# Attention: two PSUM banks for score tiles and four for chunks, the maxima of two chunks in one VectorE instruction

## What is computed

```python
# layer 0
h = _sln(hidden, w, ...)                      # layer norm, scaled and shifted by a condition
q, k, v = ...(h @ Wqkv.T + bqkv)              # 16 heads of width 32
energy = jnp.einsum('bhqd,bhkd->bhqk', q, k)
att = jax.nn.softmax(energy, axis=-1) / D ** 0.5
out = jnp.einsum('bhqk,bhkd->bhqd', att, v)
h1 = out @ Wp.T + bp + hidden
# layer 1: weights rounded to -1, 0, 1 and activations to 8 bits in the projections
attn = jax.nn.softmax(jnp.einsum('bhqd,bhkd->bhqk', q, k) * hd ** (-0.5), axis=-1)
o = jnp.einsum('bhqk,bhkd->bhqd', attn, v)
x = x + bitlinear(o, w_proj, b_proj)
x = x + bitlinear(gelu(bitlinear(adaln(x), w_fc1)), w_fc2)
```

## Time and profile before

| | |
|---|---|
| time, median of 3 runs | 2861.51 us (2854.57 to 2863.14) |
| the profiled execution | 2858.09 us |
| its span | 2856.3 us |
| TensorE products busy | 2659.4 us, 93% of the span |
| weight loads busy | 1494.5 us, 52% |
| VectorE busy | 2204.9 us, 77% |
| ScalarE busy | 1844.1 us, 65% |
| GpSimd busy | 1962.6 us, 69% |
| mean granted TensorE clock | 0.976 |

### The profile page before, as it was taken

One profiled execution on the slowest core, in us unless ns is written; L12 is line 12 of the kernel. 1 busy time (PEld: TensorE's weight loads), 2 busy tenths in 40 slices (PEclk: granted clock), 3 DMA queues, 4 the chain that ended last, 5 costly groups with the idle time before them and its releaser, 6 DMA issues. The chain is left out here.

```text
span 2856.3 us, 61816 instructions
## 1 busy us (share of the span) xinstructions
PE 2659.4 (93%) x22219; PEld 1494.5 (52%) x22273; DVE 2204.9 (77%) x4467; ACT 1844.1 (65%) x3329; POOL 1962.6 (69%) x1571
## 2 busy tenths in 40 slices
PE   7899899999999999999759998999899899959998
PEld 5655466554765547555325554554455455524444
DVE  5778678776888768877677768776878688749998
ACT  4366555665556645566456677667766776658997
POOL 0389724896269952799438987998789799965442
PEclk9999999999999999999979999999999999989999
DMA  6122443223432415223222314322332222252001
GB/s 229 39 58 63 149 123 101 58 69 133 140 94 57 121 70 166 70 62 95 74 78 60 77 32 115 80 57 45 102 79 60 69 76 58 50 205 97 33 29 38
DMA packets 102196, 243.54 MB, mean 85 GB/s; under 512 B 18828, under 2 KB 25108, under 8 KB 101016
## 3 DMA queue, kind: packets, MB, share of 16 engines
q1 hardware_dynamic: 100120, 233.49, 28.9%
q0 software_dynamic: 1792, 6.33, 0.6%
HBM read 99.15 MB, written 38.88 MB: 48 GB/s over the span
## 5 line engine op out<-in xcount | busy, mean ns | idle before, releaser
L502 DVE TENSOR_REDUCE a_mxs<-ps 128x1 f32<-128x512 f32 x2048 | 1268.5, 681 | 256.7 <-PE ps L371 254.3
L463 ACT ACTIVATE a_p<-ps 128x512 f32<-128x512 f32 x2048 | 1042.6, 607 | 202.5 <-PE ps L385 192.2
L342 POOL TENSOR_TENSOR a_sum<-a_p 128x512 f32<-128x512 f32 x768 | 985.3, 1292 | 127.3 <-PE ps L403 104.9
L371 PE MATMUL ps<-a_k,a_q 96*128 96x512 f32 x2048 | 855.0, 424 | 27.9 <-DVE a_mxs L502 24.3
L385 PE MATMUL ps<-a_q,a_k 98*128 98x512 f32 x2048 | 810.4, 419 | 18.6 <-ACT a_p L463 12.4
L347 POOL TENSOR_TENSOR a_sum<-a_sum,a_p 128x512 f32<-128x512 f32 x512 | 663.5, 1296 | 40.1
L403 PE MATMUL ps<-a_sum,a_unit 128*32 128x512 f32 x1536 | 656.4, 598 | 14.8 <-POOL a_sum L347 12.0
L403 PE MATMUL ps<-a_p,xv 128*32 128x512 f32 x3968 | 645.0, 598 | 1.4 <-DVE tok L521 1.4
L371 PEld LDWEIGHTS ps<-a_k,a_q 96*128 96x128 f32 x2048 | 388.9, 190 | 262.8 <-DVE a_mxs L502 108.8
L385 PEld LDWEIGHTS ps<-a_q,a_k 98*128 98x128 f32 x2048 | 384.2, 189 | 256.2 <-ACT a_p L463 161.7
L472 ACT ACTIVATE a_ots<-ps 128x512 f32<-128x512 f32 x256 | 152.6, 598 | 415.9 <-PE ps L403 414.7
(11 more groups left out here) (251 smaller groups left out, 3121.9 us busy)
## 6 DMA issues: line engine op xcount, KB each, us to landing
a_q<-qh SPq DMA_DIRECT2D x256, 128.0 KB, 2.3
a_k<-kh SPq DMA_DIRECT2D x256, 128.0 KB, 2.4
a_q<-ql SPq DMA_DIRECT2D x128, 128.0 KB, 2.3
a_k<-kl SPq DMA_DIRECT2D x128, 128.0 KB, 2.4
x<-a_p SPq DMA_DIRECT2D x64, 256.0 KB, 2.1
a_p<-in_w_fc SPq DMA_DIRECT2D x12, 1024.0 KB, 8.0
kh<-in_x SPq DMA_DIRECT2D x4, 2048.0 KB, 14.3
a_p<-x SPq DMA_DIRECT2D x16, 512.0 KB, 6.3
```

Source lines behind the costliest of these rows:

```text
L342: pair = pool.tensor_tensor(tile, self.key_tile(u, kt), self.key_tile(u, kt + 1), ALU.add)
L371: pe.matmul(self.mx[self.mx_ring[at]], self.q[j][0:96, t * P:(t + 1) * P], self.k[j][0:96, half * HALF:(half + 1) * HALF], start=True, sto ...
L463: act.activation(self.key_tile(u, kt), self.st[self.st_ring[CHUNKS * k + n]], ACT.Exp, scale=self.scale).then_inc(self.s_exp, 1)
L502: dve.reduce_max(self.mxs[:, k % 2, c:c + 1], self.mx[self.mx_ring[CHUNKS * k + c]], axis=AX.X).then_inc(self.s_mxr, 1)
```

## The change

The scores get two banks (0 and 1) in place of three, and each tile alternates. The chunks get four (2 to 5). The first 28 chunks of a batch still go round three of them (5, 3, 4), the later ones round all four, so that the two chunks of a step lie in neighbouring banks, 2 and 3 or 4 and 5. For those VectorE issues one reduction of a step's two chunks (`reduce_chunks`): it waits until both are there, reads 128 x 2 x 512 values across both banks, writes two columns of `mxs`, and raises `s_mxr` by two. It stands where the first of the two reductions stood, so in steps 2 (odd heads) and 6 the `divide` that stood between two reductions now stands behind the joint one. The reductions of the prelude stay single. `MX_CREDIT` grows to 32, since the bank that the early chunks don't use was last used 32 chunks ago.

```diff
--- before.py
+++ after.py
@@ -40,11 +40,12 @@
 NQ = H // NJ
 STEPS = 8
 CHUNKS = 16
-
-
-def ring(at):
-
-    return [t % 3 if t < at else (t - (2 if t == at else 1)) % 3 for t in range(H * CHUNKS)]
+EARLY_CHUNKS = 2 * (CHUNKS - 2)
+
+
+def chunk_ring():
+
+    return [(t + 2) % 3 + 1 if t < EARLY_CHUNKS else t % 4 for t in range(H * CHUNKS)]
 
 
 def back(banks):
@@ -155,7 +156,7 @@
     LD = 6 * 16
     ST_CREDIT = NJ * CHUNKS
     EXP_CREDIT = 4
-    MX_CREDIT = 4
+    MX_CREDIT = 32
     SUM = TT
     VALUES = (((0, 0), (0, 1), (0, 2), (0, SUM)), ((0, 3), (0, 4), (0, 5), (0, SUM)), ((0, 6), (0, 7), (1, 0), (0, SUM)),
               ((1, SUM), (1, 1), (1, 2), (1, 3)), ((1, SUM), (1, 4), (1, 5), (1, 6)), ((1, SUM), (2, 0), (2, 1), (1, 7)),
@@ -183,11 +184,12 @@
         self.nc, self.scale, self.out_scale, self.ident = nc, scale, out_scale, ident
         self.qh, self.ql, self.kh, self.kl = stage
         self.staged, self.values, self.tok, self.apart = staged, values, tok, apart
-        self.st_ring, self.mx_ring = ring(CHUNKS + 14), ring(2 * CHUNKS + 10)
+        self.st_ring, self.mx_ring = [t % 2 for t in range(H * CHUNKS)], chunk_ring()
         self.st_back, self.mx_back = back(self.st_ring), back(self.mx_ring)
         assert max(self.st_back) <= self.EXP_CREDIT and max(self.mx_back) <= self.MX_CREDIT
-        self.st = [ps[:, n, :] for n in range(3)]
-        self.mx = [ps[:, 3 + n, :] for n in range(3)]
+        self.st = [ps[:, n, :] for n in range(2)]
+        self.mx = [ps[:, 2 + n, :] for n in range(4)]
+        self.mx_pair = [ps[:, 2 + n:4 + n, :] for n in range(0, 4, 2)]
         self.ot = [ps[:, 6, :], ps[:, 7, :]]
         self.mt_ps = [ps[0:2 * TT, 6 + u, 256:256 + P] for u in range(2)]
         if prior:
@@ -501,6 +503,11 @@
         dve.wait_ge(self.s_mx, CHUNKS * N + c + 1)
         dve.reduce_max(self.mxs[:, k % 2, c:c + 1], self.mx[self.mx_ring[CHUNKS * k + c]], axis=AX.X).then_inc(self.s_mxr, 1)
 
+    def reduce_chunks(self, dve, N, k, c):
+
+        dve.wait_ge(self.s_mx, CHUNKS * N + c + 2)
+        dve.reduce_max(self.mxs[:, k % 2, c:c + 2], self.mx_pair[self.mx_ring[CHUNKS * k + c] // 2], axis=AX.X).then_inc(self.s_mxr, 2)
+
     def m_parts(self, dve, N, j):
         dve.wait_ge(self.s_mxr, CHUNKS * (N + 1) + self.MX_CREDIT)
         m = self.mxs[:, j % 2, :].rearrange("p (t h) -> p t h", h=2)
@@ -536,8 +543,8 @@
                 if s == 3 and k % 2 == 0 and ok(k - 1):
                     self.divide(dve, 2 * N - 2, 0, 4 * i + k - 1)
                 for c in range(2):
-                    if ok(k + a):
-                        self.reduce_chunk(dve, N + a, k + a, (2 * s + c + CHUNKS - 4) % CHUNKS)
+                    if c == 0 and ok(k + a):
+                        self.reduce_chunks(dve, N + a, k + a, (2 * s + CHUNKS - 4) % CHUNKS)
                     if s == 2 and k % 2 and c == 0 and ok(k - 1):
                         self.divide(dve, 2 * N - 2, 0, 4 * i + k - 1)
                     if s == 6 and c == 0 and ok(k - 1):
```

## The result

The changed kernel takes 3051.15 us (median of 4 runs, 3050.29 to 3052.44), the kernel before 2859.69 in the same comparison: the ratio is 1.0677, with a 95% interval of 1.066 to 1.0694. The forecast was 3055, slower. The profiled execution has a span of 3050.7 us, 194.4 more than before.

The account below looks back on a forecast made before the run. TensorE was taken to set the pace, with two score banks too few for its rate. Stretch terms of 89 + 79 + 14 + 11 + 7 - 4 = 196 us on 2858 gave 3055 us, eight-in-ten range 2975 to 3095.

Parts of the forecast that it names:

- S6 to S13, k = 1 to 13: Scores numbered 6 to 13 within a head, heads k: 104 stretches, each 0.86 us longer, 89 us.
- S14 to S5 into k = 3 to 13: Stretches of eight scores running over the end of a head: 88, each 0.90 us longer, 79 us.
- last three stretches of a batch: Stretches without chunks: 15 without other products, 11 us more; nine holding projections, 7 us more.
- k = 0: First head of a batch, 14 scores with chunks and no values between: 7.61 us with two banks, -4 us in all.
- The loop: Score bank's round from score through exponential to release, with a stall: 0.54 + 0.60 + 0.05 = 1.19 us.
- the walk: Step-by-step timing of a stretch of eight scores with two banks: ends at 4.04 us against 3.18; chance 0.70.
- rival with weights loaded ahead: A stalled score starts like one behind another product, loop 1.08 us, total 2986; chance 0.1.
- Faster by VectorE's relief: A score bank comes free early enough for two to keep up; VectorE's relief decides, about 2825 us; chance 0.04.
- hidden elsewhere: Score delay taken up by waiting value products or by time GpSimd needs anyway: 2855 to 2870 us; chance 0.02.
- the clock: Short, frequent stalls lower TensorE's clock: 940 us more if all products were hit, 3990; chance 0.02.
- So VectorE is ahead with either price: Middle stretch: pair reduced at 3.56 us (3.71 at the upper bound), before step 6's first chunk is due at 3.80.
- slower still: A second wait, at ScalarE's step 4 copy or before step 6's first chunk: 0.2 in 128 stretches, 26 us, 3081; chance 0.12.

Follow-up runs that it names:

- E1: The kernel before with only the score ring cut to two banks, chunks in three banks and single reductions: 3042.01 us, ratio 1.0642.
- E3: The changed kernel with the exponential over 384 of 512 columns, the other columns left out: 3011.43 us.
- E4: The changed kernel with the exponential over 256 of 512 columns, the other columns left out: 2981.82 us.
- E6: The changed kernel with single reductions in place of joint ones and the exponential over 256 of 512 columns: 2889.20 us, ratio 1.0113.
- E5: Control: the kernel before, three score banks, with the exponential over 256 of 512 columns: 2858.37 us, ratio 1.0006.
- E7: The changed kernel with the score ahead of its chunk in steps 3 and 7 too: 3003.65 us, ratio 1.0508.
- E2: The changed kernel with two single reductions in place of each joint one, four chunk banks kept: 3037.16 us, ratio 1.0627.

## Why the prediction was right, and where it was not

By its own terms, each summed over the starts of the score line in both traces:

| term | forecast | measured |
|---|---|---|
| S6 to S13, k = 1 to 13 | +89 | +90.7 |
| S14 to S5 into k = 3 to 13 | +79 | +84.1 |
| the same into k = 1, 2, 14 | +14 | +16.4 |
| last three stretches of a batch | +18 | +16.6 |
| k = 0 | -4 | +6.5 |
| between stretches (values) | 0 | -8.0 |
| outside the attention | 0 | -11.9 |
| sum | 196 | 194.4 |

- **The loop.** Forecast 1.19 us, and 1.20 in the timeline above. E1 shows that the bank alone does it, E3, E4 and E6 that the exponential's length is in it, E5 that with chunks it isn't in the pace with three banks, E7 that the order of products moves it as the walk says. This is shown.
- **The idle start.** The rival with weights loaded ahead (2986) is out: the released score loads its weights at 209.51 with the product, which lasts 0.51.
- **Faster by VectorE's relief, hidden elsewhere, and the clock** are out too: by E2 and E6, by the sum, and by a granted clock of 0.99 to 1.00 in seven of the eight batches' attention. In the fifth it is 0.97 (0.98 before), since its first head runs partly at 0.50, before as after.
- **The price of the pair** was right: 1.225 us measured, 1.21 forecast. The 59 us of relief were not: VectorE's busy time fell by 12. Its single reductions overlapped in the records already (1268 us for 2048), and most joint ones stand too far apart to overlap each other. With two score banks the single ones fill 1287 us (E2) and the changed kernel's 1104 + 142 = 1246, 41 less.
- **"So VectorE is ahead with either price"** failed in part. The walk checked the pair only in a middle stretch. Its sum is 1.90 + 0.43 + 1.21 = 3.54, not 3.56, and in the trace the pair starts 0.51 behind its chunk and not 0.43, so it ends at 3.63 of 3.80. That was enough from step 4 to step 6, but not over the end of a head, which is 0.07 longer than E2's. At k = 0 there are seven pairs in a row and `m_parts` among them, and there the joint reduction makes TensorE wait.
- **The term for k = 0**, -4 against +6.5, was wrong by more than that. With single reductions (E2) it is +1.1 already, so 5 of the 10.5 us are none of the pair's. The walk's 7.61 started with both banks and ScalarE free. In E2 it is 7.75 in the first layer, and in the second 8.57, since ScalarE is still at `tok` (line 1783) there and the third score waits 0.87 us for its exponential. The pair adds 5.4: 0.47 in each batch of the first layer, 0.45 in three of the second, and 2.15 in the fifth batch. That one ran at a granted clock of 0.50 for longer; whether by the pair or by chance is not shown. The first head of the changed kernel (VectorE, then TensorE):

```profile
120.64 3.63 DVE L509 TENSOR_REDUCE a_mxs<-ps 128x2 f32<-128x1024 f32 x3 [1.36 <-PE ps L373]
```

```profile
123.12 0.50 PE L373 MATMUL ps<-a_k,a_q 96*128 96x512 f32 x1 [0.18 <-DVE a_mxs L509]
```

- **The condition beside it held only roughly**: VectorE's relief "would begin to matter if the score loop were below 1.13". Far more came at 1.08 (E3) and 0.98 (E4), but a part of the 14 us was there at 1.19 already, and what matters is not the relief but the pair's lateness. The rival "slower still" had it before the first chunk of step 6, with 26 us. It isn't there (4.04 us against E2's 4.05); it is before the first chunk of step 2, with 6 us, and in the first heads.
- **The signs in the profile** that I named were half right: score starts 1.19 apart, loads 0.05 behind the exponential and products of 0.50 are there. TensorE idle at the score line is 69 us and not 150, and its share 92% and not 87%, since records of products are longer than their distance and swallow 0.17 us (0.40 less 0.235) of each stall. The wait shows in the weight loads (462 us). ScalarE's idle time before exponentials rose by 80 us (202.5 to 282.1) and not by the sum.
- **Partly by luck**: 10.5 us more at k = 0 and some 8 more in the stretches are balanced by 20 that no term had. Within the last three stretches two misses cancel as well: the 15 without projections cost 13 us and not 11, the nine with them 3 and not 7. Part of the 8 us between stretches is the last chunk's wait for VectorE: in the stretch from S6 it started 0.31 us behind its score before and starts 0.25 behind it now (in the other 0.24 and 0.23). Of the 12 us outside the attention 5.8 lie between the third batch and the fourth, where the granted clock was 0.95 before and 0.99 after, so about half comes with the clock of this one execution before. The rest is not explained.

## What to carry to other kernels

Price a ring of buffers by its loop, write to release with the idle start in it, over the number of banks, and compare that with the producer's own distance: here 1.19 over 3 was under 0.47 and 1.19 over 2 over it, and that one division told that the change would lose; the walk then gave the 7%. Two reductions joined into one save some 0.06 us of VectorE (two joint ones back to back start 2.36 - 1.22 = 1.14 apart in E4, single ones 0.60) and cost the head start of the first: a reduction that works behind a producer with few buffers should start on the first tile. A busy share of 77% is not a reserve where the consumer's own distance (0.60) is longer than the producer's (0.47) within a burst. And a total that stays the same, as in E5, is not yet a control: look at the stretches that the edit could touch.

## What was not expected of the hardware

- A joint reduction over two banks starts 0.50 us after the start of its second product, a single one 0.44 (medians over those that found VectorE idle, the single ones behind a product that streamed).
- The granted clock held at 0.99 to 1.00 through stalls of 0.2 to 0.3 us every 1.2 us, in seven of eight batches' attention. It stood at 0.50 in the first head of the fifth batch, both before and after: it fell while TensorE stood waiting for 2 to 3 us near that head's start. The Trainium skill ("TensorE: Matmul & The Clock Gate", section "A second HAM failure mode: psum-queue depth-cycling") describes a kernel where such idling made it go up and down. The measurements here differ from that: the mean granted clock is 0.975 after and 0.976 before.
